# Attention's set-up in another order: normalisation and projection weights in front, later slots' clearings and lambdas behind the opening turn

## The reference, cut to what matters

```
x = x + 0.5 * ffn(layernorm(x))        # mixture of 8 experts, the best 2 per token
x = x + attention(layernorm(x))        # differential attention, 16 heads of 8
x = x + 0.5 * ffn(layernorm(x))

# attention
q = x @ Wq.T + bq ; k = x @ Wk.T + bk ; v = x @ Wv.T + bv      # q, k: two halves per head
q1, q2, k1, k2 = rope(...)                                      # rotary embedding
a1 = softmax(causal(q1 k1 * scale)) ; a2 = softmax(causal(q2 k2 * scale))
lam = 0.2 + exp(sum(lq1 * lk1)) - exp(sum(lq2 * lk2))           # one number per head
out = (a1 - lam * a2) @ v
out = rmsnorm(out) * head_norm_w * 0.8 ; return out @ Wo.T + bo
```

## Time and profile before

| | us |
|---|---|
| median of 3 runs | 1847.65 (1845.17 to 1851.52) |
| the profiled execution: its own time | 1848.93 |
| its span | 1847.2 |
| first feed-forward layer | about 0 to 436 |
| attention | about 436 to 1400 |
| second feed-forward layer | about 1400 to 1847 |
| PE busy | 1617.2 (88%) |

### The profile page before, as it was taken

One profiled execution on the slowest core, in us unless ns is written; L12 is line 12 of the kernel. 1 busy time (PEld: TensorE's weight loads), 2 busy tenths in 40 slices (PEclk: granted clock), 3 DMA queues, 4 the chain that ended last, 5 costly groups with the idle time before them and its releaser, 6 DMA issues. The chain is left out here.

```text
span 1847.2 us, 43588 instructions
## 1 busy us (share of the span) xinstructions
PE 1617.2 (88%) x16768; PEld 1235.7 (67%) x16768; DVE 1340.0 (73%) x3034; ACT 1199.2 (65%) x1581; POOL 1318.8 (71%) x836
## 2 busy tenths in 40 slices
PE   4999999994379998988989988998872799999998
PEld 3787778783256666666666666666652588778787
DVE  5777777764578887888888788888732677777775
ACT  4777777772156676676666666666662577777776
POOL 4888888875447677777767767767633688888885
PEclk9999999997689999999999999999985899999999
DMA  3333233232222322332332332332202233233231
GB/s 114 104 115 113 84 103 115 104 104 52 77 59 80 96 83 66 96 89 65 92 88 70 85 83 72 89 92 68 80 17 71 98 115 105 88 106 115 104 110 63
DMA packets 143678, 163.16 MB, mean 88 GB/s; under 512 B 13244, under 2 KB 125582, under 8 KB 142478
## 3 DMA queue, kind: packets, MB, share of 16 engines
q1 hardware_dynamic: 143472, 160.38, 28.4%
HBM read 91.20 MB, written 14.70 MB: 57 GB/s over the span
## 5 line engine op out<-in xcount | busy, mean ns | idle before, releaser
L292 POOL TENSOR_TENSOR ffn_h_low<-ffn_h,ffn_h_high 128x1024 fp32r<-128x1024 f32 x192 | 458.7, 2402 | 95.1 <-ACT ffn_h_high L341 94.9
L1047 ACT ACTIVATE att_prob<-att_ring 128x1024 f32<-128x1024 f32 x384 | 390.2, 1023 | 182.6 <-PE att_ring L1277 182.0
L1153 DVE TENSOR_REDUCE att_nmax<-att_ring 128x4 f32<-128x1024 f32 (+1 forms) x384 | 453.2, 1215 | 41.1 <-PE att_ring L1277 38.4
L479 DVE TENSOR_TENSOR ffn_h<-ffn_up,ffn_comb_wide 128x1024 f32<-128x1024 f32 x256 | 311.1, 1215 | 126.1 <-ACT ffn_up L334 125.9
L334 ACT ACTIVATE ffn_up<-ffn_up 128x1024 f32<-128x1024 f32 x256 | 258.1, 1008 | 202.2 <-PE ffn_up L567 200.7
L341 ACT ACTIVATE ffn_h_high<-ffn_h 128x1024 fp32r<-128x1024 f32 x256 | 269.4, 1052 | 0.7 <-DVE ffn_h L479 0.7
L971 POOL TENSOR_TENSOR att_rrms<-att_ms_eps,att_minus_halves 128x32 f32<-128x32 f32 x32 | 174.0, 5439 | 68.0 <-DVE att_ms_eps L1179 68.0
L1277 PE MATMUL att_ring<-att_qs,att_kd 64*128 64x256 bf16 (+1 forms) x2048 | 153.9, 250 | 74.4 <-DVE att_nmax L1153 23.3
L567 PE MATMUL ffn_up<-ffn_xt_high,ffn_w_high 128*128 128x512 f32 x512 | 214.7, 419 | 1.7 <-DVE ffn_h L479 1.7
L284 POOL TENSOR_TENSOR ffn_ez<-ffn_e_const,ffn_nz 128x16 f32<-128x16 f32 x64 | 185.6, 2901 | 38.2 <-DVE ffn_nz L405 38.2
L580 PE MATMUL ffn_y<-ffn_h_high,ffn_w_high 128*128 128x512 f32 x512 | 205.4, 401 | 6.4 <-POOL ffn_h_low L292 5.3
(11 more groups left out here) (152 smaller groups left out, 3242.7 us busy)
## 6 DMA issues: line engine op xcount, KB each, us to landing
ffn_comb_wide<-ffn_comb_d SPq DMA_DIRECT2D x128, 512.0 KB, 5.6
att_qs<-att_parts SPq DMA_DIRECT2D x192, 128.0 KB, 2.4
att_kd<-att_parts SPq DMA_DIRECT2D x192, 128.0 KB, 2.4
ffn_x<-x SPq DMA_DIRECT2D x32, 256.0 KB, 3.1
ffn_w<-w SPq DMA_DIRECT2D x4, 1024.0 KB, 7.4
x<-ffn_out SPq DMA_DIRECT2D x16, 256.0 KB, 2.4
att_x<-x SPq DMA_DIRECT2D x32, 128.0 KB, 2.3
att_xr<-x SPq DMA_DIRECT2D x32, 128.0 KB, 2.3
```

The source lines that it names most:

```text
L292: nc.gpsimd.tensor_tensor(hts[1][:, e % NH], h[:, e % NH], hts[0][:, e % NH], ALU.subtract).then_inc(low_by_pool, 1)
L479: nc.vector.tensor_tensor(h[:, e % NH], up[:, e % NUP], comb_wide[:, b.c % NW, e].unsqueeze(1).to_broadcast([P, HE, FT]), ALU.mult).then_i ...
L1047: nc.scalar.activation(prob[:, u % NP], ring[:, ORDER.index((kind, u)) % 3], ACT.Exp, scale=SCALE).then_inc(prob_ready, 1)
L1153: nc.vector.tensor_reduce(nmax[:, b, :, h0:h0 + cnt], ring[:, pos % 3] .rearrange("p (s h k) -> p s h k", s=2, k=width), AX.X, ALU.max, ne ...
```

## The change

The same instructions run in another order, with finer semaphores. wqk has its own semaphore `wqk_in`; rope and bqk have `rope_in` and are issued ahead of wv and wo; the other nine loads keep `weights_in`, and whoever waits for it now waits for all nine. POOL makes `ident` first, raises the variance as soon as DVE has it, and clears slots 1 and 2 of `qs` behind turn -1. ACT normalises before it rounds weights, and computes the lambdas' Exp behind turn -1. DVE makes the low part of wqk right behind the first `clear_keys`, `biased` after it, and the lambdas behind turn -1. PE waits before its first turn for `ident` and the low part of wqk alone, and for masks, `v` and the nine loads behind it.

```
@@ SP
-                for name, dst in (("wqk", wqk), ("bqk", bqk), ("wv", wv), ("wo", wo), ("rope", rope)):
+                sp.dma_start(wqk[:], w["wqk"]).then_inc(wqk_in, 16)
+                for name, dst in (("rope", rope), ("bqk", bqk)):
+                    sp.dma_start(dst[:], w[name]).then_inc(rope_in, 16)
+                for name, dst in (("wv", wv), ("wo", wo)):
                     sp.dma_start(dst[:], w[name]).then_inc(weights_in, 16)
...
-                sp.wait_ge(setup, 2)
+                sp.wait_ge(setup, 3)
@@ POOL
                 nc.gpsimd.memset(ident[:], 0.0)
+                nc.gpsimd.memset(minus_half[:], -0.5).then_inc(setup, 1)
+                pool.wait_ge(setup, 1)
+                nc.gpsimd.affine_select(out=ident[:], ...).then_inc(setup, 1)
...
+                ln_rstd(Turn(-2))
+                pool.wait_ge(halves_step, 1)
...
-                nc.gpsimd.memset(v[:], 0.0).then_inc(setup, 1)
-                nc.gpsimd.memset(minus_halves[:], -0.5).then_inc(minus_set, 1)
-                pool.wait_ge(minus_set, 1)
-                pool.wait_ge(setup, 3)
-                nc.gpsimd.memset(v[:, :, :, :, HD:HD + 1], 1.0).then_inc(v_set, 1)
...
                 clear_queries(0)
+                nc.gpsimd.memset(v[:], 0.0).then_inc(setup, 1)
+                pool.wait_ge(setup, 4)
+                nc.gpsimd.memset(v[:, :, :, :, HD:HD + 1], 1.0).then_inc(v_set, 1)
...
-                ln_rstd(Turn(-2))
+                first = Turn(-1)
+                pool.wait_ge(bias_step, 2)
+                body(first)
                 clear_queries(1)
                 clear_queries(2)
-                pool.wait_ge(dve_setup, 1)
-                pool.wait_ge(weights_in, 16 * 12)
-                pool.wait_ge(bias_step, 2)
-                turns(body, -1)
+                pool.wait_ge(weights_in, 16 * 9)
+                pool.wait_ge(lam_step, 5)
+                turns(body, 0)
@@ ACT
-                act.wait_ge(weights_in, 16 * 12)
-                nc.scalar.activation(wqks[0][:], wqk[:], ACT.Copy).then_inc(weight_high, 1)
-                nc.scalar.activation(wvs[0][:], wv[:], ACT.Copy).then_inc(weight_high, 1)
-                act.wait_ge(lam_sums, 1)
-                nc.scalar.activation(lam_exp[:], lam_sum[:], ACT.Exp).then_inc(lam_ready, 1)
...
                 normalise(Turn(-2))
-                turns(body, -1)
+                act.wait_ge(wqk_in, 16)
+                nc.scalar.activation(wqks[0][:], wqk[:], ACT.Copy).then_inc(weight_high, 1)
+                act.wait_ge(weights_in, 16 * 9)
+                nc.scalar.activation(wvs[0][:], wv[:], ACT.Copy).then_inc(weight_high, 1)
+                body(Turn(-1))
+                act.wait_ge(lam_step, 2)
+                nc.scalar.activation(lam_exp[:], lam_sum[:], ACT.Exp).then_inc(lam_ready, 1)
+                turns(body, 0)
@@ DVE (the lambda lines move, with their waits, from here to behind clear_keys(2))
                 clear_keys(0)
+                dve.wait_ge(weight_high, 1)
+                nc.vector.tensor_tensor(wqks[1][:], wqk[:], wqks[0][:], ALU.subtract).then_inc(weight_low, 1)
+                dve.wait_ge(rope_in, 32)
...
                 dve.wait_ge(weight_high, 2)
-                nc.vector.tensor_tensor(wqks[1][:], wqk[:], wqks[0][:], ALU.subtract).then_inc(weight_low, 1)
                 nc.vector.tensor_tensor(wvs[1][:], wv[:], wvs[0][:], ALU.subtract).then_inc(weight_low, 1)
+                dve.wait_ge(weights_in, 16 * 9)
                 dve.wait_ge(v_set, 1)
                 body(first.after())
                 clear_keys(1)
                 clear_keys(2)
@@ PE
-                te.wait_ge(dve_setup, 1)
                 te.wait_ge(setup, 2)
-                te.wait_ge(v_set, 1)
-                te.wait_ge(masks_in, 16 * 4)
                 tile = [slice(TILE * s, TILE * (s + 1)) for s in range(2)]
-                te.wait_ge(weights_in, 16 * 12)
-                te.wait_ge(weight_low, 2)
+                te.wait_ge(weight_low, 1)
...
                             elif kind == "V":
+                                if turn.c == -1:
+                                    te.wait_ge(weight_low, 2)
...
-                turns(body, -1)
+                body(Turn(-1))
+                te.wait_ge(setup, 3)
+                te.wait_ge(v_set, 1)
+                te.wait_ge(masks_in, 16 * 4)
+                te.wait_ge(weights_in, 16 * 9)
+                turns(body, 0)
```

More of the change, by code:

```diff
@@ L781, in attention @@
         v_set = sem("v_set")
-        minus_set = sem("minus_set")
+        wqk_in = sem("wqk_in")
+        rope_in = sem("rope_in")
         lam_ready = sem("lam_ready")
-        lam_sums = sem("lam_sums")
         lam_step = sem("lam_step")
@@ L900, in _ @@
                 nc.gpsimd.memset(ident[:], 0.0)
+                nc.gpsimd.memset(minus_half[:], -0.5).then_inc(setup, 1)
+                pool.wait_ge(setup, 1)
+                nc.gpsimd.affine_select(out=ident[:], in_=ident[:], compare_op=ALU.not_equal, fill=1.0,
+                                        base=0, pattern=[[-1, P]], channel_multiplier=1).then_inc(setup, 1)
                 nc.gpsimd.memset(eye[0:TILE], 0.0)
@@ L903, in _, with ln_rstd @@
                 nc.gpsimd.memset(hide_t[0:TILE], 0.0)
+                nc.gpsimd.memset(minus_halves[:], -0.5)
                 nc.gpsimd.memset(halves[0:2, 0], MASKED)
[L905 to L909, removed]
+                nc.gpsimd.memset(halves[0:2, 1], 1.0).then_inc(halves_step, 1)
+                def ln_rstd(turn):
+                    wait(pool, ln_step, turn.at(2, 3, 3))
+                    wait(pool, xn_ready, turn.at(1, 1, 1))
+                    nc.gpsimd.tensor_tensor(rstd[:], var_eps[:], minus_half[:], ALU.pow).then_inc(rstd_ready, 1)
+                ln_rstd(Turn(-2))
+                pool.wait_ge(halves_step, 1)
                 for half in range(2):
@@ L928, in _ @@
                 last.then_inc(setup, 1)
[L930 to L934, removed]
                 def low_part(turn, n, what):
@@ L1240, in _, with by_head @@
                 clear_keys(2)
+                for n in range(2):
+                    last = nc.vector.tensor_tensor(lam_prod[:, n], lam_in[:, 2 * n], lam_in[:, 2 * n + 1], ALU.mult)
+                last.then_inc(lam_step, 1)
+                dve.wait_ge(lam_step, 1)
+                nc.vector.tensor_reduce(lam_sum[:], lam_prod[:].rearrange("p n (h d) -> p n h d", d=HD), AX.X,
+                                        ALU.add).then_inc(lam_step, 1)
+                nc.vector.memset(stream_w[:, :, 0], 1.0).then_inc(lam_step, 1)
+                def by_head(n):
+                    return lam_exp[:, n].rearrange("p (g x) -> p g x", x=2)
+                nc.vector.tensor_scalar(norm_w[:], norm_w[:], 1.0 - LAMBDA_INIT, None, ALU.mult).then_inc(lam_step, 1)
+                dve.wait_ge(lam_ready, 1)
+                nc.vector.scalar_tensor_tensor(out=stream_w[:, :, 1], in0=by_head(1), scalar=-LAMBDA_INIT,
+                                               in1=by_head(0), op0=ALU.add, op1=ALU.subtract).then_inc(lam_step, 1)
+                dve.wait_ge(lam_step, 5)
                 turns(body, 0)
```

20 lines of the change are left out of this document (2 added, 18 removed).

## The result

| | before | changed kernel |
|---|---|---|
| median of 7 runs | 1847.65 us (1845.17 to 1854.84) | 1837.91 us (1836.16 to 1844.34) |
| ratio to before | | 0.995 (95%: 0.9933 to 0.9967) |
| profiled execution: own time, span | 1848.93, 1847.2 | 1844.34, 1842.6 |

The change made the kernel faster, by 9.2 us by the ratio (6.1 to 12.4). The two profiled executions stand 4.6 us apart. The start of attention, which is all that the change touches, gained the same to 0.2 us in both executions of it that were traced, so I read that first. Its positions are counted from the issue of attention's first load, 436.34 us before and 436.16 after.

What follows compares the result with a forecast made beforehand. It took attention's start-up, a 9.2 us chain from last load to QK 0, as the only place to save: profiled 1848.93 less 8.0 is 1840.9, standing 1.28 above the median, so 1839.7 us; range 1835.3 to 1845.

Steps and rivals of the forecast that it cites:

- The bound: Attention's start-up: only there can the change save; steady turns stay untouched, and S 0 moves with QK 0.
- Normalisation and low part of wqk: Start of attention: rstd near 440.5, xn near 441.6, transposes at 444.1, all beside the loads and off the path.
- What ends last now: Start of turn -1: last lambda load at 447.68, then wv_high and xt_high; QK 0 at 448.9, 8.0 us earlier.
- A rule against the change: DVE beside POOL in the start: wqk_low holding up POOL's last selection would cut the gain to 7.1; none taken, 8.0.
- POOL's new order: POOL before turn -1: v_set at 448.0, hidden by 0.3 us ahead of xt_low at 448.3; memsets not slowed.
- The edits behind turn -1: Moved clearings and lambda rows (1.87 us) cost nothing; xt_low of turn 0 hidden by 1.5 us; masks 0.4 later.
- The clock: PE's first QK matmuls at 1.2 GHz: QK 0 cannot get slower; an earlier rise could save about half of 2.5 us.
- The time: Whole kernel: profiled 1848.93 less 8.0 is 1840.9; median predicted at 1839.7 us.
- Rival (c): Steady turns settle at a lower granted clock: a 0.02 fall costs 16.4 us, time 1856; chance 0.04.
- (a): Start moves less or part is given back: gain under 5.5 us, time about 1843.5; chance 0.11.
- (b): Gain above 8: loads land earlier, 1839.4, or 1837 with earlier clock rise; small terms within the forecast's 0.85.
- (d): Wait for nine loads ahead of xt_high remains: gain 8.0, not about 11; priced in, no separate chance.

Runs made afterwards that it cites:

- wv_own_semaphore: Changed kernel with wv counted with rope and bqk, so ACT rounds it without waiting for the lambda loads; QK 0 at 14.64 us, against 14.46 in the changed kernel.
- biased_behind_xt: Changed kernel with the eight biased instructions moved on DVE behind xt_low of turn -1; median 1842.74 us, ratio 0.9975, QK 0 at 12.84 us.
- the mended version: Changed kernel with wv counted with rope and bqk, biased behind xt_low, later waits, and most of POOL's v clearing moved later; median 1837.26 us, ratio 0.9946 to before.

## Why the prediction was right, and where it was not

**The bound.** Right: only the start of attention moved, and S 0 followed QK 0 (they moved by 6.05 and 6.11). From there on the kernels differ by scatter alone, as the table's last column shows.

**Normalisation and low part of wqk.** Right. `rstd` 3.15 us into attention (3.4 predicted), `xn` at 4.16 (4.4), the transposes at 7.89 (7.8).

**"What ends last now."** This step failed. I let the start end with the landing of the last load, `wv_high` and `xt_high`, and QK 0 at 448.9 follow. `xt_high` did end at 448.53, but `biased`, taken at its old 2.88 us up to the next row, took 6.0 (443.87 to 449.86), and DVE reached `xt_low` 1.5 us later than its operand was ready. The term that was wrong is the length of `biased` beside POOL's memsets; the price was 1.9 us at QK 0. The start gained 6.1, not 8.0. `wv_own_semaphore` shows that the load was not the bound, `biased_behind_xt` that it would have been one without the hold-up.

**"A rule against the change".** This is where that length was decided, and it was decided wrongly. I weighed the right pair of engines the wrong way round. I asked how long a DVE instruction could hold POOL, and found 1.23 us at most; the cost was a POOL memset that held DVE. I also drew "at no cost" from memset beside memset, which says nothing of a tensor_scalar. The row that did was in the trace of before, on DVE's timeline, and I had not read it:

```profile
449.55 0.51 DVE L1216 TENSOR_SCALAR att_norm_w<-att_norm_w 128x128 f32<-128x128 f32 x1
```

0.51 us for 128 elements per partition, ended at 450.06, beside POOL's clearings that end at 449.98. Where POOL is idle, in the changed kernel, the same instruction has 0.21 on the same timeline:

```profile
472.26 0.21 DVE L1243 TENSOR_SCALAR att_norm_w<-att_norm_w 128x128 f32<-128x128 f32 x1
```

Nor do the rows show company at no cost throughout, as the prediction had it. Further on in the trace of before, DVE's second shift and POOL's low part, which both read SBUF, end together, and the shift took 1.11 us where the first took 0.16 (DVE's timeline, then POOL's):

```profile
472.02 1.11 DVE L1117 SCALAR_TENSOR_TENSOR att_shift<-att_mean_var,att_rstd 128x2 f32<-128x2 f32 x1 [8.01 <-POOL att_rstd L934]
471.96 1.15 POOL L953 TENSOR_TENSOR att_parts<-att_left,att_parts 128x512 bf16<-128x512 f32 x1
```

The Trainium skill ("SBUF — State Buffer", Who interferes with whom) has it: a `tensor_scalar` can run in a VectorE mode that takes both ports, and of it and a GpSimd instruction "Whoever issues first gets the shared pair for the whole instruction". The other is blocked until then. The prediction drew on this section for instructions with two operands and passed over this line. The trace agrees, and adds that back-to-back memsets on POOL act as one (5.3 us of clearings and 2.65 of `v`, one hold-up of 6.99). It also agrees in a second place: `wqk_low`, which reads two SBUF operands, took 1.59 us instead of 1.23 in each kernel in which it stood beside POOL's last selections, which read SBUF, and 1.23 in each in which it did not. That 0.36 was hidden in the change, and lies on the path of the mended version.

**POOL's new order.** Right as to itself: `v_set` was there 11.4 us into attention (11.7 predicted), and POOL's memsets kept their lengths. Wrong in calling it hidden: nothing waited for the memsets, and yet they stretched an instruction that was on the path.

**The edits behind turn -1.** Right. The lambda rows took 1.34 us (I had 1.87), `xt_low` of turn 0 ended 2.3 us before QK 0 needed it, POOL's two clearings kept 3.55 and nobody waited for them. The masks went out 0.1 us later than before; I had expected 0.4.

**The clock.** QK 0 ran at 1.2 GHz as before, and the stretch from the old 455 to 481 had 0.57 in both kernels (stretches of the changed kernel, columns as in the earlier trace rows). That it "cannot get slower" holds for QK 0 alone. The first matmul with a short row came 6.2 us behind QK 0's start, at 456.81, where it was 4.0 before, so QK 1 ran at the low level throughout; the second `turned` followed the first by 2.55 us instead of 1.99. The chain through POOL hid it: S 0 lost 0.06 of the gain.

```profile
447.00:473.00 26.00, 7.13 (x32) 6.64 (x32) 12.87 (x29) 5.76 (x11) 14.24 (x13) 0.57 0.23 64
...
522.00:1342.00 820.00, 736.08 (x12152) 536.19 (x12154) 665.66 (x964) 538.32 (x767) 571.67 (x464) 0.98 0.29 81
```

**The time.** The measured 1837.91 lies 1.8 under the predicted 1839.7 and inside the range, but not because the sum was right: the start gave 6.1 of the 8.0, and the first set of runs fell well, which is luck. The table's last column says why sets differ. From S 0 on all ten kernels run the same instructions in the same order, and that stretch took 931.0 to 936.7 us with no relation to the edit. A turn usually takes 26.84 us, and others take 27.2 to 31.3, as here the turn that starts at 910 beside its neighbour (columns as in the earlier trace rows):

```profile
883.00:910.00 27.00, 24.57 (x410) 17.93 (x409) 22.61 (x33) 18.13 (x26) 19.88 (x17) 1.00 0.30 85
910.00:941.00 31.00, 26.93 (x409) 19.27 (x408) 21.89 (x33) 18.33 (x26) 19.44 (x17) 0.89 0.26 71
```

In the long turn the granted clock fell, 0.89 against 1.00. But PE had by then stood idle since 922.97 for a DMA, the one that brings the rows of maxima into `qs`, and the fall came inside that wait, at 924.4; the neighbour has no such row:

```profile
925.43 0.61 PE L1280 MATMUL att_ring<-att_qs,att_kd 64*128 64x256 bf16 x4 [2.46 <-DMA att_qs<-att_max_rows]
```

The transfer ahead of it (`att_max_rows<-att_nmax_t`) landed 3.7 us after its issue in this turn and 1.5 in the neighbour. So it is in all ten traces, before included: of their 260 turns from the projection of sequence 5 on, 119 took 27.2 or more, at nearly the same places in every kernel, and in 115 of these PE had waited 1.0 to 2.6 us for that DMA. The clock fell in 45 turns, all of them long ones (28.8 to 31.3); the long turns without a fall took 27.2 to 28.4. Which of the long turns have a fall differs from execution to execution, and with it the length of the stretch: 931.0 us with 3 falls, 935.7 with 7 and 936.7 with 6, though 5 falls went with 931.6 as well as with 936.2. That the wait makes the clock fall, and why the transfer lands late in just these turns, no run tested. Rival (c) named the clock; its steady loss did not come. The 0.98 above against 0.99 before is the end of the start-up, in which the clock was low until 531.9: from 532 to 1342 the changed kernel has 0.99. But the noise of the clock is several microseconds, more than the 2 us of straying that I allowed. The two sets of runs (9.2 and 3.9 us) agree with what the start shows, about 6 us.

**The rivals.** (a), a gain under 5.5, is nearer than I had it: the 1.9 us lost at QK 0 are most of the 2.5 that it needed, only by another mechanism than the two I priced. (b) did not come. (d) was right in seeing unused room: the mended version took it, 6.0 us more at QK 0 than the change.

## What to carry to other kernels

When a reorder fills an idle stretch, list what runs beside what on VectorE and GpSimd, not only what waits for what: an instruction that is off the path can stretch one that is on it. Before taking a duration from a row, look for the same operation's shortest and longest row and for what the other engine did meanwhile; a tensor_scalar with a long row beside a GpSimd memset is the sign. The hold-up shows as a long row, not as idle time, so a view of waits misses it. Put clearings on GpSimd where VectorE does reductions, memsets, tensor_tensor or nothing, and let them wait for the tensor_scalars to be done. And when executions scatter by more than the change is worth, compare turns of one trace: here the long ones cost 16 to 24 us in every kernel, more than this whole start-up gave.

## What the runs showed of the hardware

- A GpSimd memset holds a VectorE tensor_scalar (float32, SBUF to SBUF) until the last of the back-to-back memsets ends: 3.50 us, 6.99 us and, for `norm_w`, 4.00 us were the longest held rows. What stands behind it on VectorE waits too (0.18 became 3.04). Every held instruction here began while a memset was running; the reverse order was not tried.
- VectorE's memset (1.76 us), scalar_tensor_tensor (four in 1.67 us), tensor_tensor (two in 0.42) and tensor_reduce (0.42) kept their lengths beside GpSimd memsets, and GpSimd's memsets (2.65 and 1.80) kept theirs beside all.
- A tensor_tensor of two SBUF operands took 1.59 us instead of 1.23 beside a GpSimd selection that reads SBUF, and a scalar_tensor_tensor of 128x2 took 1.11 instead of 0.16 beside a GpSimd tensor_tensor.
- TensorE's granted clock fell in the middle of attention (45 falls in ten traces) only in turns of 28.8 us and more, in 44 of them beside a wait of 1.2 to 2.6 us for a DMA.
